# One look at low halves of weights in each quarter in place of two, and the first two rows' statistics apart

## The reference

```
q, k, v = (x @ (codes * repeat(scales, 32)) + bias) for wq, wk, wv      # 512 -> 16 heads x 128
x = layernorm(x + softmax(q k^T / sqrt(128)) v @ (wo_codes * scales) + bo)
x = layernorm(x + cross attention of x to ctx (2 x 1024 x 512), the 54 largest scores kept)
x = layernorm(x + (silu(x Wg) * (x Wu)) @ Wd)                           # 512 -> 2048 -> 512
```

## Time and profile before

| | |
|---|---|
| Median of 3 runs | 911.99 us (911.7 to 912.0) |
| The profiled execution's own time | 911.83 us |
| Its span, first to last instruction | 910.0 us |
| Busy: TensorE, its weight loads | 900.3 us (99%), 747.6 us (82%) |
| Busy: VectorE, ScalarE, GpSimd | 588.6, 582.6, 498.5 us (65%, 64%, 55%) |
| Looks, L1144 | 68, 0.62 us each |
| Totals, L2152 | 30 |
| GpSimd's idle time before totals that ended with a look | 81.7 us |

### The profile page before, as it was taken

How to read it: one execution, slowest core, us unless ns; L and a number is a source line. 1 busy time by engine, 2 the same in 40 slices (tenths; PEclk the granted TensorE clock), 3 DMA queues, 4 the chain that set the end, 5 groups by cost and what they waited for, 6 DMA issues and landing times.

```text
span 910.0 us, 13246 instructions
## 1 busy us (share of the span) xinstructions
PE 900.3 (99%) x4440; PEld 747.6 (82%) x4440; DVE 588.6 (65%) x1057; ACT 582.6 (64%) x1161; POOL 498.5 (55%) x413
## 2 busy tenths in 40 slices
PE   9999999999999999999999999999999999999997
PEld 7888788888888888888778888998888888888885
DVE  5767966678667687676696999987797125511114
ACT  5667976688767788678875686634656535533333
POOL 4258742656515576477784677726574833345540
PEclk9999999999999999999999999999999999999999
DMA  6531330122300322222131213423433431333321
GB/s 209 163 106 57 90 91 1 44 80 76 91 15 30 94 76 58 66 78 74 47 115 47 71 48 96 125 70 114 129 110 96 121 92 55 122 113 104 90 74 46
DMA packets 46102, 76.97 MB, mean 85 GB/s; under 512 B 5584, under 2 KB 11216, under 8 KB 45776
## 3 DMA queue, kind: packets, MB, share of 16 engines
q1 hardware_dynamic: 45888, 76.00, 28.6%
q10 hardware_dynamic: 144, 0.07, 0.0%
HBM read 73.69 MB, written 2.36 MB: 84 GB/s over the span
## 4 chain that ended last, share of the span: by engine, by line
PE 86%; DVE 8%; issue 2%; ACT 1%; POOL 1%; DMA 0%; SPq 0%; DVEq 0%; POOLq 0%; ACTq 0%
PE p L1004 6%; PE p L1008 6%; PE p L1005 6%; PE p L746 6%; PE p L783 5%; PE p L748 4%; PE p L728 3%; PE p L1018 3%; PE p L724 3%; PE p L1019 3%; PE p L1020 3%; PE p L726 3%; PE p L793 3%; PE p L797 3%; PE p L794 3%; PE p L768 3%
## 5 line engine op out<-in xcount | busy, mean ns | idle before, releaser
L2172 POOL TENSOR_TENSOR V<-RAW,V 128x512 fp32r<-128x512 f32 x64 | 81.7, 1299 | 129.7 <-ACT V L1190 129.7
L1658 DVE TENSOR_SCALAR_CACHE_REDUCE JK<-p,ssc 128x512 bf16<-128x512 f32 x112 | 83.6, 747 | 98.4 <-PE p L728 98.3
L1131 ACT ACTIVATE PR<-p,nms,ssc 128x512 f32<-128x512 f32 x112 | 87.3, 780 | 59.5 <-DVE JK L1658 58.7
L2167 POOL TENSOR_TENSOR acc<-SX,acc 128x512 f32<-128x512 f32 x56 | 72.8, 1300 | 60.1 <-ACT SX L1170 34.9
L746 PE MATMUL p<-R 128*128 128x512 f32 x248 | 97.3, 392 | 0.1
L2172 POOL TENSOR_TENSOR C<-RAW,C 128x512 fp32r<-128x512 f32 x58 | 76.8, 1333 | 27.9 <-ACT C L1190 27.8
L1671 DVE TENSOR_TENSOR PT<-p,PT 128x512 fp32r<-128x512 f32 x128 | 87.3, 682 | 3.0 <-ACT PT L1150 2.9
L2001 DVE TENSOR_TENSOR SX<-p,SX 128x512 f32<-128x512 f32 x32 | 22.0, 689 | 99.8 <-PE p L1008 90.5
L783 PEld LDWEIGHTS p<-ident,PR 128*128 128x128 f32 x512 | 63.5, 140 | 17.2 <-DVE PT L1671 0.9
L783 PE MATMUL p<-ident,PR 128*128 128x128 f32 x512 | 76.7, 272 | 0.2 <-ACT PR L1131 0.2
L1150 ACT ACTIVATE PT<-p 128x512 fp32r<-128x512 f32 x128 | 75.9, 593 | 0.0
(11 more groups left out here) (251 smaller groups left out, 2716.4 us busy)
## 6 DMA issues: line engine op xcount, KB each, us to landing
RAW<-in_wg SPq DMA_DIRECT2D x32, 256.0 KB, 2.9
RAW<-in_wu SPq DMA_DIRECT2D x32, 256.0 KB, 2.6
RAW<-in_ctxn SPq DMA_DIRECT2D x32, 256.0 KB, 2.8
RAW<-in_wd SPq DMA_DIRECT2D x32, 256.0 KB, 2.8
RAW<-in_wq SPq DMA_DIRECT2D x19, 256.0 KB, 2.6
RAW<-in_wk SPq DMA_DIRECT2D x19, 256.0 KB, 2.7
RAW<-in_wv SPq DMA_DIRECT2D x16, 256.0 KB, 3.4
RAW<-in_wo SPq DMA_DIRECT2D x16, 256.0 KB, 3.3
```

Source lines behind the costliest of these rows:

```text
L1131: e.activation(PR[:, i % 2, :], P[i % 2][:, :], ACT.Exp, bias=nms[:, i % 4:i % 4 + 1], scale=ssc[:, 0:1] if HB[j][0] > 1 else SC, accum_ou ...
L1658: e.tensor_scalar(JK[:, :], P[i % 2][:, :], ssc[:, 1:2] if HB[i // 4][0] > 1 else -SC, None, ALU.mult, ALU.min, accum_out=nms[:, i % 4:i % ...
L2172: e.tensor_tensor(lo, RAW[:, slot[key], :], hi, ALU.subtract).then_inc(*c_lo.up(key))
```

## The change

In `low_plan` the plan takes up to two pieces from the queue in each of the steps up to 3, as before, and one piece in each step from 4 on. And the statistics of rows 0 and 1 are issued apart, row 0 at the end of VectorE's step 116 and row 1 at the end of step 117; rows 2 and 3 stay together in step 119.

```
@@ low_plan
-        for _ in range(2):
+        for _ in range(2 if i < 4 else 1):
             if queue and queue[0][0] < max(i, 0):
                 piece = queue.pop(0)[1]
...
@@ vector
-                if (j, qt) == (29, 1):
-                    ln_stats(1, [0, 1], row_writers(0)[-6])
+                if j == 29 and qt < 2:
+                    ln_stats(1, [qt], row_writers(qt)[-6])
                 if (j, qt) == (29, 3):
                     ln_stats(1, [2, 3], row_writers(2)[-6])
```

## The result

The changed kernel takes 915.52 us (median of 6 runs, 914.17 to 916.30) against 911.93 us for the kernel before (6 runs beside it): ratio 1.0037, 95% interval 1.0027 to 1.0048. It is slower by 3.6 us, above the range of 911.0 to 915.0. Its profiled execution took 915.89 us with a span of 914.1, so 4.1 us more span than before.

What follows compares the result with a forecast made beforehand. The prediction took TensorE, busy 900.3 of 910.0 us, as the bound. It added 1.7 (step 112, gain included) + 0.3 (late flags) - 0.15 (statistics) = 1.85 to 911.83, forecasting a median of 913.8 us, range 911.0 to 915.0.

Steps and rivals of the forecast that it cites:

- Steps 28, 60, 92: Flags of heads 8, 16 and 24's query and key weights lose their cover: 0.1 us each, 0.3 us for three.
- Steps 110 and 111: With step 108's pair of looks parted, TensorE's score matmuls around 433 us no longer wait: 0.67 us gained.
- Step 112, the wait: Flag of (qk, 29) comes late, TensorE stands still 2.4 us; +1.7 us with the 0.67 us gain inside.
- The statistics: Rows 0 and 1 split on VectorE, steps 116 to 120: add of row 2 starts earlier, net 0.15 us won.
- the bank of the transposes: Around 460.99 us, freed later since the low half of PT(117) comes later: TensorE loses 0.1 us there.
- (o, 6)'s last look: One more piece for ScalarE at the end of step 103, before a long step with an attend: no cost.
- the clock as a rival of 0.05: Clock falls to 1.2 GHz at step 112's rest, costing 1.0 us more: 914.8 us; chance 0.05.
- The sum: Whole kernel: 1.7 + 0.3 - 0.15 = 1.85 us on the profiled 911.83 gives 913.7; as a median 913.8.
- That 1.7 us at step 112 would be absorbed later: Lagging engines at 471 to 475 us take up most of the wait: net 0 to +1.2, 912.5 us; chance 0.15.
- Faster: Flag of (qk, 29) not late, 0.67 us won, TensorE's queue at 462 to 475 us cleared: 910.0 us; chance 0.12.
- Totals piled up on GpSimd: Flag totals late by 0.5 us in each of steps 28, 60, 92 and 2.2 at 112: 915.4 us; chance 0.08.

Runs made afterwards that it cites:

- half_104: Kernel before with one look per quarter from step 104 on and five matmuls, result unread, ahead of the load of (qk, 29)'s flag; 913.67 us.
- best: Kernel before with statistics parted, one look in step 108 alone, step 109's two looks exchanged, VectorE's (o, 14) and (o, 15) bias additions at step 107's end; 910.78 us.
- bias_later: Changed kernel with VectorE's two bias additions of (o, 14) and (o, 15) moved to the end of step 107; 914.95 us, ratio 1.0032.
- looks_only: Changed kernel with the statistics of rows 0 and 1 kept together; 915.79 us, ratio 1.0049 against the kernel before.

## Why the prediction was wrong

**Steps 28, 60, 92: right.** +0.1 each was forecast, 0.09 to 0.11 came. The look stands behind PT as worked out, and the weights follow late by "issue". ScalarE and TensorE's weight loads, step 27, changed kernel (answers to the earlier trace rows):

```profile
124.25 0.59 ACT L1150 ACTIVATE PT<-p 128x512 fp32r<-128x512 f32 x1
124.73 0.63 ACT L1144 ACTIVATE JA<-R 128x512 bf16<-128x512 f32 x1
```

```profile
126.31 0.19 PEld L746 LDWEIGHTS p<-R 128*128 128x128 f32 x1 [0.22 <-issue]
```

**Steps 110 and 111: right.** -0.67 forecast, -0.69 measured, and -0.67 to -0.71 in the ten other kernels that part the pair of step 108.

**Step 112, the wait: right.** Forecast were a rest of 2.4 us behind a total that stands behind a multiply, ending at 437.4, and a matmul at 437.8. Less the 0.83 us by which this profile runs late at step 108, the rows read 437.3 and 437.85.

**The statistics: right in sum, wrong in the working.** -0.15 forecast, -0.2 measured. One row costs VectorE 0.82 us and not 0.75, and TensorE loses 0.31 at step 119 and not 0.1. VectorE and then TensorE, changed kernel (answers to the earlier trace rows):

```profile
462.50 0.68 DVE L1691 BATCH_NORM_STATS2 st<-acc 128x6 f32<-128x512 f32 x1
463.21 0.18 DVE L1694 BATCH_NORM_AGGREGATE mv<-st 128x2 f32<-128x6 f32 x1
463.32 0.75 DVE L1658 TENSOR_SCALAR_CACHE_REDUCE JK<-p,ssc 128x512 bf16<-128x512 f32 x1
463.99 0.08 DVE L1658 DVE_READ_ACCUMULATOR JK<-p,ssc 128x1 f32 x1
463.99 0.74 DVE L1644 SCALAR_TENSOR_TENSOR QK<-p,bqk_t,QK 128x512 fp32r<-128x512 f32 x1
```

```profile
464.34 0.40 PE L726 MATMUL p<-QK 128*128 128x512 f32 x1
464.79 0.50 PE L728 MATMUL p<-QK 128*128 128x512 f32 x1
```

It is the low half of QK behind the maximum that is late, so the third score matmul comes 0.45 behind the second and not 0.23; the bank of the transposes, which was named, isn't it. The gain at step 120 is larger by as much.

**Failed: "(o, 6)'s last look gives ScalarE one more piece at the end of step 103, before a long step with an attend: nothing."** It costs 0.53 us, five steps on. The prediction asked whether (o, 6)'s flag would be late and whether ScalarE had room. It didn't ask what else leaves ScalarE's queue behind the look: the high halves at 412.32 (411.41 before), on which GpSimd's low halves and SP's next two loads wait, the scales of out among them. ScalarE and SyncE, the kernel before and then the changed one:

```profile
411.41 1.14 ACT L1106 ACTIVATE R<-RAW 128x512 fp32r<-128x512 f32 x2
413.80 0.59 SPq L544 DMA_DIRECT2D SCL<-in_so  x1
```

```profile
411.71 0.62 ACT L1144 ACTIVATE JA<-WO 128x512 bf16<-128x512 f32 x1
412.32 1.14 ACT L1106 ACTIVATE R<-RAW 128x512 fp32r<-128x512 f32 x2
414.72 0.59 SPq L544 DMA_DIRECT2D SCL<-in_so  x1
```

Less the 0.3 us by which all rows are late there, the delay is 0.62 us at the high halves, 0.62 in the issue of the scales and 0.55 at the multiply that waits for them, and there it meets a VectorE that has none to spare.

**Failed: the clock as a rival of 0.05, priced at 1.0 us.** The mechanism was named, and its place; chance and size were wrong. The price was taken from the slow stretch at the start of the kernel, 8 matmuls in 1.83 us. Here the slow stretch is 3.4 us long and costs 1.6. The chance was taken from the longest rest in the trace, 1.03 us. A row of 1.03 us says nothing of a rest of 2.4, and half_104, with a rest of 1.07 us and a clock of 1.00, shows how little. The Trainium skill, "TensorE: Matmul & The Clock Gate", section "Why this matters for your kernels", warns that rests between bursts can bring TensorE back to its low clock; three of five traces with the rest agree, with 0.51 to 0.52 granted behind it. The page's row is on longer rests than these 2.3 us; what was measured decides.

**The sum.** 0.33 + 0.53 - 0.69 + 2.5 - 0.2 = 2.5 without the clock, 914.4 us, in the range; 4.1 with it, 916.0, outside. So the clock is the term that carries the time out of the range, and (o, 6)'s look alone would not have. The six runs stand around these two values: 914.17, 914.54 and 915.16 with a mean clock of 1.000, 915.88, 915.89 and 916.30 with 0.996 to 0.998. The median lies in the gap between the two groups; it belongs to neither, and with one fallen clock less in six it would have been about 914.9, inside the range.

**The rivals.** That 1.7 us at step 112 would be absorbed later (0.15): no, the shift stays constant to the end. Faster (0.12): no, though best shows that the gain exists once the flag keeps its cover. Totals piled up on GpSimd (0.08): the time came out near its 915.4, but for other reasons; the total of 0.73 us that spoke for it is GpSimd's side of the clash with VectorE at step 108, and in bias_later and best, where that is gone, the longest of the 30 totals takes 0.33 us.

## What to carry to other kernels

When a piece is moved in an engine's queue, follow what stands behind it through the next engine and the load queue, and not only who wants the piece's result: a look of 0.6 us cost 0.5 us five steps later. Price a rest of TensorE like this one (2.3 us) as its own length and, with a fair chance, the slow stretch behind it (1.6 us here); if the rest can't be avoided, some matmuls of 512 columns in it, whose result nothing reads, are worth having (1.0 to 1.5 us here for five or ten). Keep flags that a sequencer reads early: swapping two looks took a wait of 0.28 us away at no cost.

## What the runs showed of the hardware

- The granted clock fell to 0.51 to 0.52 for some 3.4 us behind rests of 2.3 us in three of five profiles. In the changed kernel it fell only 1.3 us after TensorE had gone back to work at 0.23 us a matmul (438.68 to 439.92); in looks_only the first matmul behind the rest (438.17, 0.77 us) was slow already. With a rest of 1.07 us or none at the same place it stayed at 1.00, and so it did in the kernel before.
- VectorE's additions with two SBUF inputs (line 1866, 0.74 us alone) ended 0.55 us after the end of the GpSimd operation beside which they started, in all 11 such cases of the profile before, from 85 to 424 us; the GpSimd operation queued next was stretched in turn (from 1.29 to as much as 1.75 us, a total from 0.32 to 0.78). The Trainium skill, "SBUF — State Buffer", section "SBUF: two separate sides", says that such a VectorE operation and a GpSimd operation share a pair of ports by an exclusive lock, so that the later one stands still until the other is through. The traces agree that the later one is held up; but the addition ends 0.55 us after the other's end and not 0.74, so some 0.2 us of it isn't.
- The scales' load of out took 5.55 to 6.18 us from its issue to the multiply that waits for it, in 14 profiles; one profile alone doesn't tell such a variation from an effect of an edit.
